# Feature and output rows written pair by pair from ScalarE's queue, gate logits made by node, and the last groups' VectorE steps in another order

## Chip, core and metric

The kernel runs on one core of one Trainium2 chip. The metric is the device time of one execution in microseconds (us). The profile of the kernel before is one execution of 2493.28 us, whose recorded span is 2491.6 us; the 1.7 us between them lie around the span.

## The reference

Three layers work on 6250 nodes with 256 features each: a graph convolution over 200,000 edges, a linear-attention block, and a mixture of eight experts. Only the last matters for the change. In short:

```python
xn = layernorm(x)
x = x + relu(gcn(edges, xn, W, b)) + mix(xn)          # called x2 in the kernel
h = layernorm(x)
logits = h @ gate_w + gate_b                          # 8 numbers per node
probs = softmax(logits); idx = argmax(probs)          # the expert of every node
pos = running count of the nodes of the same expert   # its place in the expert's list
kept = pos < 977                                      # 1.25 * 6250 / 8
y = relu(h @ w1[idx] + b1[idx]) @ w2[idx] + b2[idx]
out = x + y * probs[idx] * kept
```

## The kernel before

Nodes lie in 49 blocks of 128 (one node on each partition); the last block is partly padding. `acc` and `res` hold a block each in `[:, b, :]`.

**Edge stage.** 1563 chunks of 128 edges are processed in units of four. GpSimd gathers the source rows of a chunk with one indirect DMA (`ring<-node_rows,src_chunk`, L1026), SyncE counts a unit as ready when its rows have landed, TensorE multiplies it with a selection matrix (an item, L1087, two parts with other work between them), and VectorE adds the product to its block (`add`, L1662). An item is a unit and a block; there are 439. The last 49 items, numbered j = 0 to 48, each complete one block.

**Routing, inside those last 49 items.** As block b is complete, VectorE makes x2 (`x2`, L1809) and its statistics. For each pair t of blocks TensorE transposes x2 (`turn(t)`, L1204), ScalarE copies the result to `xT` (`copy`, L1458), and TensorE makes the gate logits. Before, these came out by expert (8 partitions by 256 nodes, `logits`, L1214), ScalarE copied them (`logits_out`, L1464), and TensorE transposed them to nodes (`logits_by_node`, L1224). ScalarE also scales x2 by dinv into `res` (`scale`, L1491); `res` then holds acc times dinv, 256 numbers, and three columns more of every node (`C:ROW`): minus mean over deviation, the inverse deviation, and the expert's probability.

Blocks are in groups, `RB = [0, 14, 28, 42, 49]`, group 0 to 3. For each group VectorE takes six `normal` steps (ending in two of the columns), eight `choose` steps (the expert), two `counted`, two `probability` steps (they need ScalarE's `exponent`, L1485, and end in the third column) and six `assign` steps: `cur`, `place`, `slot`, high and low part, `one_hi`, `one_lo`, `node_of`. `assign` needs the counts from TensorE (`places`, L1237 to L1245), and is followed there by `owners` (L1257), which puts node numbers into lists by expert. The steps of group g are taken at fixed gaps between the adds of group g+1; the table `STEPS` has the gap of each (28 gaps with 14 blocks, 14 gaps with the last 7). Gap 2u stands ahead of the add of block u of the group, 2u+1 behind its x2. After the last add, group 3's own steps follow, with `assign` of group 2 between its `normal` steps. VectorE then turns the lists into row numbers (`slots_ok`, L2094 to L2101).

**Writes.** Rows of 259 numbers go to `node_features` (`rows_out`, group 0 and 1 from ScalarE's queue at L1564, group 2 and 3 from SyncE's at L993); x2 rows go to the output (`x2_out`, groups 0 to 2 from ScalarE's queue at L1570, group 3 from SyncE's, L999, after the first four gathers of expert 0). `dma_out` and `dma_x2` count them.

**Expert stage.** GpSimd waits for `slots_ok` and for all of `dma_out`, and gathers expert 0's rows in eight DMAs (`load_rows(0)`, L1034). Then it waits for all of `dma_x2`, sets paddings to zero (L1043 to L1046, counted by `pads`), since two of these tiles lie where `acc` and `res` were, and gathers expert 1's rows. TensorE transposes rows 0 to 3 (`transposes`, L1284), makes the first two blocks of products of expert 0 (L1302) from the first half of its rows with the transposes of rows 4 to 7 between, and waits for `pads` ahead of the third block. From there to the end the eight experts run in one chain of TensorE, ScalarE and VectorE.

## Time and profile before

| | before |
|---|---|
| three runs, median (lowest to highest) | 2497.04 us (2495.24 to 2499.4) |
| profiled execution, its own time | 2493.28 us |
| its span | 2491.6 us |
| TensorE / TensorE weight loads busy | 1891.6 us (76%) / 1490.8 us (60%) |
| GpSimd busy | 1689.7 us (68%) |
| VectorE busy | 1210.4 us (49%) |
| ScalarE busy | 826.8 us (33%) |

Busy times are sums over the whole span and overlap each other. The edge stage takes the time to about 2058 us; the expert stage starts with GpSimd's first row gather at 2090.52 us and goes on to the end. The change works between these two points and around them.

### The profile page before, as it was taken

What the parts mean: (1) busy time and instruction counts of PE and PEld (TensorE: products, weight loads), DVE (VectorE), ACT (ScalarE), POOL (GpSimd) and SP (SyncE); (2) the same over time, 40 slices, a digit from 0 to 9 for tenths busy, and PEclk for the clock granted to TensorE, in tenths of its full rate; (3) what the DMA queues carried; (4) which work ended last, traced back from release to release, by engine and by line L of the source; (5) the groups of instructions that cost most, each with busy time, mean ns of one, the idle gap of its engine ahead of it and who ended that gap; (6) DMA issues with size and microseconds to landing.
All of it is one profiled execution on the core that took longest, in us unless ns stands there. A gap on an engine that the chain in (4) does not pass through costs nothing. (4 is left out here: it accounts for less than half of the span.)

```text
span 2491.6 us, 33433 instructions
## 1 busy us (share of the span) xinstructions
PE 1891.6 (76%) x8818; PEld 1490.8 (60%) x8818; DVE 1210.4 (49%) x3211; ACT 826.8 (33%) x1649; POOL 1689.7 (68%) x1780
## 2 busy tenths in 40 slices
PE   8588888677676776676777777777767775999997
PEld 7355555556555555555565555555544443998997
DVE  6333322344444444444444444444334554887886
ACT  5322222133333333233333333233201224565653
POOL 6577777777777777777777777777777772333432
PEclk9798999888988988889888888888879887999999
DMA  7433333333333333333333333333334446222320
GB/s 236 149 105 106 104 106 106 106 105 105 106 106 105 105 106 106 106 106 105 105 106 106 105 106 106 106 105 106 106 106 134 127 154 185 78 66 87 91 76 9
DMA packets 128044, 270.94 MB, mean 109 GB/s; under 512 B 33576, under 2 KB 71428, under 8 KB 127738
## 3 DMA queue, kind: packets, MB, share of 16 engines
q0 software_dynamic: 82992, 221.52, 31.0%
q1 hardware_dynamic: 35834, 38.11, 4.9%
q10 hardware_dynamic: 9040, 9.22, 1.2%
q8 instruction: 78, 1.28, 0.2%
q14 instruction: 100, 0.82, 0.1%
HBM read 244.15 MB, written 27.35 MB: 109 GB/s over the span
## 5 line engine op out<-in xcount | busy, mean ns | idle before, releaser
L1026 POOL DMA_INDIRECT ring<-node_rows,src_chunk x1563 | 1485.4, 950 | 491.7 <-issue 475.8
L1087 PE MATMUL p_item<-ring,sel 128*128 x3512 | 1010.4, 428 | 537.9 <-SPq L973 487.9
L1087 PEld LDWEIGHTS p_item<-ring,sel 128*128 128x128 f32 x3512 | 691.3, 210 | 767.9 <-issue 686.7
L1662 DVE TENSOR_TENSOR acc<-acc,p_item 128x256 f32 (+1 forms) x439 | 183.5, 418 | 620.0 <-PE p_item L1087 616.1
L1644 DVE SCALAR_TENSOR_TENSOR sel<-dst_chunk,nbase,p_col 128x512 f32<-128x512 f32 x439 | 326.5, 744 | 54.9 <-issue 36.9
L1052 POOL DMA_INDIRECT out_dram<-oo,slot_node x64 | 75.1, 1173 | 225.5 <-DVE oo L2006 222.6
L1391 ACT ACTIVATE x1T<-p_t,col_ln1b,col_ln1g 128x128 f32<-128x128 f32 x98 | 39.5, 453 | 333.7 <-PE p_item L1087 333.7
L1398 ACT ACTIVATE gT<-p_t,col_b 128x128 f32<-128x128 f32 x98 | 30.6, 363 | 315.0 <-PE p_item L1087 315.0
L1742 DVE SCALAR_TENSOR_TENSOR kf<-p_q,ke 128x256 f32<-128x256 f32 x49 | 20.8, 424 | 222.6 <-ACT ke L1373 222.6
L1034 POOL DMA_INDIRECT rows<-node_features,slot_row x64 | 73.0, 1141 | 54.7 <-DMA node_features<-res 35.7
L1150 PE MATMUL p_q<-wq_sb,xnT_m 128*128 128x512 f32 x196 | 108.6, 682 | 0.3
L1366 ACT ACTIVATE yn<-p_q 128x256 f32<-128x256 f32 x49 | 18.8, 383 | 228.2 <-PE p_item L1087 228.2
L1124 PEld LDWEIGHTS p_t<-x1T,w1t_sb 128*128 128x128 f32 x392 | 74.4, 266 | 5.4
L1302 PE MATMUL p_item<-bTh,w1h 128*128 128x490 f32 (+1 forms) x192 | 74.6, 389 | 4.0 <-DVE bTl L1953 2.1
L1423 ACT COPY xnT_m<-p_t 128x256 f32<-128x256 f32 x49 | 18.2, 372 | 176.2 <-PE p_item L1087 176.2
L2014 DVE TENSOR_TENSOR hTl<-hbuf,hTh 128x978 fp32r<-128x978 f32 x64 | 75.4, 1178 | 2.2
L1316 PE MATMUL p_col<-w2h,hTh 128*128 128x256 f32 x256 | 75.6, 295 | 0.8 <-DVE hTl L2014 0.7
L1316 PE MATMUL p_y<-w2h,hTh 128*128 128x256 f32 x256 | 74.7, 292 | 0.0
L1302 PE MATMUL p_item<-bTh,w1l 128*128 128x490 f32 (+1 forms) x192 | 74.3, 387 | 0.0
L1302 PE MATMUL p_item<-bTl,w1h 128*128 128x490 f32 (+1 forms) x192 | 73.8, 385 | 0.0
L1124 PE MATMUL p_t<-x1T,w1t_sb 128*128 128x128 f32 x392 | 73.5, 350 | 0.0
L1316 PE MATMUL p_y<-w2h,hTl 128*128 128x256 f32 x256 | 72.5, 283 | 0.0
(276 smaller groups left out, 3239.1 us busy)
## 6 DMA issues: line engine op xcount, KB each, us to landing
ring<-node_rows,src_chunk POOLq DMA_INDIRECT x1563, 2.8
w1raw<-in_w SPq DMA_DIRECT2D x8, 1024.0 KB, 5.4
w2raw<-in_w SPq DMA_DIRECT2D x8, 1024.0 KB, 6.7
res<-in_x SPq DMA_DIRECT2D x7, 896.0 KB, 9.7
out_dram<-res ACTq DMA_DIRECT2D x3, 1792.0 KB, 11.1
node_rows<-acc SPq DMA_DIRECT2D x4, 1024.0 KB, 4.9
node_features<-res ACTq DMA_DIRECT2D x2, 1813.0 KB, 9.7
node_features<-res SPq DMA_DIRECT2D x1, 1813.0 KB, 10.4
```

What stands on the lines that cost most here:

```text
L1026: nc.gpsimd.indirect_dma_start(ring[:, c % RING // U, c % U, :], None, table, bass.IndirectOffsetOnAxis(src_chunk[:, c:c + 1], 0)).then_in ...
L1034: nc.gpsimd.indirect_dma_start(rows[0:r, e % 2, t, :], None, feats, bass.IndirectOffsetOnAxis(slot_row[0:r, k:k + 1], 0)).then_inc((gather ...
L1052: nc.gpsimd.indirect_dma_start(out, bass.IndirectOffsetOnAxis(slot_node[0:r, k:k + 1], 0), oo[0:r, t % 2, :], None, bounds_check=N - 1, oo ...
L1087: mm = pe.matmul(p_item[bank(i)][:, 0:C], sel[:, i % SELR, u, :], rows[:, u, :], start=(u == 0), stop=(u == U - 1), skip_group_check=True)
L1124: pe.matmul(p_t[:, m, :], w1t_sb[:, a, m * P:(m + 1) * P], x1T[:, a, :], start=(a == 0), stop=(a == CH - 1))
L1150: pe.matmul(p_kv, xnT[:, a, :], wq_sb[:, a, C:3 * C], start=(a == 0), stop=(a == CH - 1))
L1302: mm = pe.matmul(e_f[c % 4][:, 0:NH[h]], w[:, a, j * P:(j + 1) * P], b[:, a, h * NH[0]:h * NH[0] + NH[h]], start=(q == 0), stop=(q == len( ...
L1316: mm = pe.matmul(e_y[t % 2][:, 0:C], h[:, j, t * P:(t + 1) * P], w[:, j, :], start=(q == 0), stop=(q == len(parts) - 1))
L1391: nc.scalar.activation(x1T[:, a, :], p_t[:, a, :], ACT.Identity, scale=g["cols"]["ln1g"][:, a:a + 1], bias=g["cols"]["ln1b"][:, a:a + 1]). ...
L1644: nc.vector.scalar_tensor_tensor(sel[:, i % SELR, :, :], dst.rearrange("p (u e) -> p u e", e=1).broadcast_to([P, U, P]), nbase[:, bass.ds( ...
L1662: nc.vector.tensor_tensor(a, a, p_item[bank(j)][:, 0:C], ALU.add).then_inc(added, 1)
L2014: V.tensor_tensor(hTl[:, j, 0:CAPE], hbuf[:, j % NBUF, :], hTh[:, j, 0:CAPE].bitcast(F32), ALU.subtract).then_inc(lo_ok, 1)
```

## The change

1. **Writes.** The 256 scaled numbers of a row and its three columns are written apart. Pairs 0 to 19 (blocks 0 to 39) go from ScalarE's queue, right behind their `scale`, each as two DMAs of 256 rows of 1024 bytes: to `node_features` and to the output. Blocks 40 to 43 and 44 to 48 go to `node_features` from SyncE's queue. The three columns go in one DMA for each group (12 bytes a node), group 0 and 1 from ScalarE's queue, 2 and 3 from SyncE's. The output rows of blocks 40 to 48 (before: 42 to 48) go from SyncE after all eight gathers of expert 0 (before: four).
2. **Logits.** Each block's transposed x2 is the stationary side of the matmul, with the gate weights (8 columns) moving, so that logits come out by node; the copy and the second transpose go.
3. **Order.** `STEPS` changes, `places(2)` moves ahead of TensorE's last item, and `assign` of group 2 moves ahead of VectorE's last add. `places` stands ahead of an item, not inside it. ScalarE takes `root` ahead of `scale`, group 2's `exponent` two pairs sooner, and `node_low(2)` ahead of the last scales.
4. **Waits.** ScalarE's wait for `dma_out` and `dma_x2` moves from the start of expert 0 to its first copy of w2; VectorE gets the same wait ahead of expert 0.

```diff
-    PLACES_AT = [RB[gi + 1] + 9 for gi in range(NG - 2)]
+    LATE_PAIR = 20
+    NFEAT, NX2 = LATE_PAIR + NG + 2, LATE_PAIR + 1
+    PLACES_AT = [min(RB[gi + 1] + 9, NBLK - 1) for gi in range(NG - 1)]
-        14: ((0, 1, 2, 3, 4, 5), (7, 8, 8, 9, 9, 10, 10, 11), (12, 12), (13, 13), ()),
+        14: ((0, 3, 4, 4, 5, 6), (6, 6, 7, 7, 8, 8, 8, 9), (10, 10), (13, 13), (12, 12, 12, 12, 12, 12)),
...
             sp.wait_ge(multiplied, NITEM)
-            rows_out(NG - 2)
+            rows_out(2 * LATE_PAIR, NBLK - 5)
             load_w2(sp, 0)
...
-            rows_out(NG - 1)
-            for t in range(RT // 2):
+            columns_out(NG - 2)
+            rows_out(NBLK - 5, NBLK)
+            columns_out(NG - 1)
+            for t in range(RT):
                 sp.wait_ge(gathered[t], rows_gathered(t) + 16)
-            x2_out(NG - 1)
+            sp.dma_start(out[2 * LATE_PAIR * P:NBLK * P, :].rearrange("(b p) c -> p b c", p=P),
+                         res[:, 2 * LATE_PAIR:NBLK, 0:C]).then_inc(dma_x2, 16)
...
             pool.wait_ge(slots_ok, 2)
-            pool.wait_ge(dma_out, 16 * NOUT)
+            pool.wait_ge(dma_out, 16 * NFEAT)
             load_rows(0)
-            pool.wait_ge(dma_x2, 16 * NOUT)
+            pool.wait_ge(dma_x2, 16 * NX2)
...
                 for i, b in enumerate(blocks_of(t)):
                     u = b - RB[gi]
-                    pe.transpose(p_l[:, u * EXP:(u + 1) * EXP], lgT[:, t % 2, i * P:(i + 1) * P],
-                                 ident[0:EXP, 0:EXP]).then_inc(l_ps, 1)
+                    for a in range(CH):
+                        mm = pe.matmul(p_l[:, u * EXP:(u + 1) * EXP], xT[:, t % XT, i * CH + a, :], gate_sb[:, a, :],
+                                       start=(a == 0), stop=(a == CH - 1))
+                    mm.then_inc(l_ps, 1)
...
+            def x2_out(t):
+
+                lo, hi = blocks_of(t)[0], blocks_of(t)[-1] + 1
+                s.wait_ge(scaled, hi)
+                s.dma_start(feats[lo * P:hi * P, 0:C].rearrange("(b p) c -> p b c", p=P), res[:, lo:hi, 0:C]
+                            ).then_inc(dma_out, 16)
+                s.dma_start(out[lo * P:hi * P, :].rearrange("(b p) c -> p b c", p=P), res[:, lo:hi, 0:C]
+                            ).then_inc(dma_x2, 16)
+
+            def columns_out(gi):
 
                 s.wait_ge(cols_ok, 3 * gi + 3)
-                s.wait_ge(scaled, RB[gi + 1])
-                s.dma_start(feats[RB[gi] * P:RB[gi + 1] * P, :].rearrange("(b p) c -> p b c", p=P),
-                            res[:, blocks(gi), :]).then_inc(dma_out, 16)
+                with nc.allow_non_contiguous_dma("three numbers of every node"):
+                    s.dma_start(feats[RB[gi] * P:RB[gi + 1] * P, C:ROW].rearrange("(b p) c -> p b c", p=P),
+                                res[:, blocks(gi), C:ROW]).then_inc(dma_out, 16)
...
+            node_low(NG - 2)
             scale(NPAIR - 2)
             scale(NPAIR - 1)
-            node_low(NG - 2)
...
                 normal(NG - 1, i)
-                assign(NG - 2, i)
...
+            v.wait_ge(dma_out, 16 * NFEAT)
+            v.wait_ge(dma_x2, 16 * NX2)
             all_experts(v, expert)
```

VectorE, from its last add (L1662) on, in the kernel before. `psum_e` is the first `probability` step of group 2, `veps` the first `normal` step of group 3, `cur` and `place_r` are the first `assign` steps of group 2, `inv` is group 3's.

```order
L1662 TENSOR_TENSOR acc<-acc,p_item 128x256 [waits added,multiplied]
L1814 BN_STATS stt<-acc 128x6 [waits r_x2]
L1818 BN_AGGR mvg<-stt 128x2 [waits r_bn]
L1809 SCALAR_TENSOR_TENSOR acc<-acc,res 128x256 [waits added]
L1895 TENSOR_REDUCE psum_e<-ex 128x14 [waits r_eact]
L1898 RECIPROCAL res<-psum_e 128x14 [waits r_dv]
L1814 BN_STATS stt<-acc 128x6 [waits r_x2]
L1818 BN_AGGR mvg<-stt 128x2 [waits r_bn] x2
L1826 SCALAR_TENSOR_TENSOR veps<-deg_1199,mvg 128x7 [waits r_dv]
L1906 TENSOR_TENSOR cur<-oh,p_nd 128x112 [waits r_oh,r_cum]
L1829 RECIPROCAL inv<-sdg 128x7 [waits r_std]
L1910 TENSOR_REDUCE place_r<-cur 128x14 [waits r_dv]
```

VectorE in the changed kernel, from the x2 of block 47 on. The add is the same one, now at L1650.

```order
L1894 TENSOR_TENSOR cur<-oh,p_nd 128x112 [waits r_oh,r_cum]
L1898 TENSOR_REDUCE place_r<-cur 128x14 [waits r_dv]
L1901 SCALAR_TENSOR_TENSOR slot_r<-place_r,m_1208 128x14 [waits r_dv]
L1905 TENSOR_SCALAR slot_hi<-slot_r 128x14 [waits r_dv]
L1906 TENSOR_SCALAR slot_lo<-slot_r 128x14
L1910 TENSOR_TENSOR one_hi_r<-col,slot_hi 128x896 [waits r_mapped,r_dv]
L1913 TENSOR_TENSOR one_lo_r<-col,slot_lo 128x1792
L1916 TENSOR_TENSOR node_of<-one_hi_r,node_hi 128x14x64 [waits r_onehi]
L1650 TENSOR_TENSOR acc<-acc,p_item 128x256 [waits added,multiplied]
L1802 BN_STATS stt<-acc 128x6 [waits r_x2]
L1806 BN_AGGR mvg<-stt 128x2 [waits r_bn]
L1797 SCALAR_TENSOR_TENSOR acc<-acc,res 128x256 [waits added]
```

All of group 2's `assign` steps now stand ahead of the last add; before, the first came after it, and behind `veps` of group 3.

ScalarE, from the copy of the last transposes on, in the kernel before. `sdg` is `root(3)`, `node_of` is `node_low(2)`, `ex` is `exponent(3)`, and an ACT_TABLE_LOAD changes the function table.

```order
L1458 COPY xT_r<-p_t 128x256 [waits r_lt,r_turned]
L1464 COPY lgT<-p_item 8x256 [waits r_lps,r_lt]
L1480 ACT_TABLE_LOAD
L1480 ACTIVATE sdg<-veps 128x7 [waits r_var]
L1464 COPY lgT<-p_item 8x128 [waits r_lps,r_lt]
L1491 ACTIVATE res<-acc,dinv 128x256 [waits r_x2] x3
L1471 ACTIVATE node_of<-one_hi_r,node_lo 128x14x64 [waits r_mapped,r_onehi]
L1511 CAST w1h<-w1raw 128x512 [waits d_w1,multiplied]
L1485 ACT_TABLE_LOAD
L1485 ACTIVATE ex<-ex 128x56 [waits r_e]
```

ScalarE in the changed kernel, at the same place.

```order
L1452 COPY xT_r<-p_t 128x256 [waits r_lps,r_turned]
L1468 ACT_TABLE_LOAD
L1468 ACTIVATE sdg<-veps 128x7 [waits r_var]
L1459 ACTIVATE node_of<-one_hi_r,node_lo 128x14x64 [waits r_mapped,r_onehi]
L1479 ACTIVATE res<-acc,dinv 128x256 [waits r_x2] x3
L1499 CAST w1h<-w1raw 128x512 [waits d_w1,multiplied]
L1473 ACT_TABLE_LOAD
L1473 ACTIVATE ex<-ex 128x56 [waits r_e]
```

Two copies of logits are gone; `node_low(2)` stands ahead of the three scales.

SyncE after the last unit, in the kernel before (`w1raw` there is expert 1's).

```order
L993 DMA node_features<-res 128x14x259 [waits multiplied,r_scaled,r_cols]
L960 DMA w2raw<-in_w 128x8x256
L1005 DMA fb_b<-in_fb 128x2048
L993 DMA node_features<-res 128x7x259 [waits r_scaled,r_cols]
L999 DMA out_dram<-res 128x7x256 [waits gathered3,gathered2,r_scaled,gathered1,gathered0]
L957 DMA w1raw<-in_w 128x2x1024 [waits e_w1l]
```

SyncE in the changed kernel, at the same place.

```order
L994 DMA node_features<-res 128x4x256 [waits multiplied,r_scaled]
L962 DMA w2raw<-in_w 128x8x256
L1007 DMA fb_b<-in_fb 128x2048
L1001 DMA node_features<-res 128x14x3 [waits r_cols]
L994 DMA node_features<-res 128x5x256 [waits r_scaled]
L1001 DMA node_features<-res 128x7x3 [waits r_cols]
L1014 DMA out_dram<-res 128x9x256 [waits gathered4,gathered5,gathered3,gathered6,gathered2,gathered7,gathered1,gathered0]
L959 DMA w1raw<-in_w 128x2x1024 [waits e_w1l]
```

The last feature write of 7 whole rows is now 5 rows and 7 times three numbers, and the output write waits for four more gathers.

## Rows read from the trace of the kernel before

**Rows 1.** The page's costliest groups: the gathers of the edge stage (columns in the page's order)

```profile
L1026 POOL DMA_INDIRECT ring<-node_rows,src_chunk x1563 | 1485.4, 950 | 491.7 <-issue 475.8
```

**Rows 2.** Timeline: two gathers and TensorE's item behind each, an output write (start, us)

```profile
1855.20 0.95 POOL L1026 DMA_INDIRECT ring<-node_rows,src_chunk  x1 [0.30 <-issue]
...
1858.16 2.07 PE L1087 MATMUL p_item<-ring,sel 128*128 x4 [1.97 <-SPq L973]
...
2052.74 0.38 ACTq L1570 DMA_DIRECT2D out_dram<-res  x1
...
2053.90 0.95 POOL L1026 DMA_INDIRECT ring<-node_rows,src_chunk  x1 [0.30 <-issue]
...
2058.50 2.07 PE L1087 MATMUL p_item<-ring,sel 128*128 x4 [5.94 <-SPq L973]
```

**Rows 3.** Stretches: busy time of each engine, granted TensorE clock, DMA share, GB/s

```profile
2054.00:2058.00 4.00, 0.00 (x0) 0.00 (x0) 0.94 (x5) 0.00 (x0) 0.85 (x1) 0.67 1.05 275
2058.00:2062.00 4.00, 3.50 (x8) 1.55 (x8) 0.00 (x0) 0.00 (x0) 0.00 (x0) 0.50 1.08 391
```

**Rows 4.** Timeline from the x2 of block 47 to the first row gather

```profile
2065.05 0.40 DVE L1809 SCALAR_TENSOR_TENSOR acc<-acc,res 128x256 f32<-128x256 f32 x1
...
2066.76 0.42 DVE L1662 TENSOR_TENSOR acc<-acc,p_item 128x256 f32<-128x256 f32 x1 [0.54 <-PE p_item L1087]
...
2067.52 0.39 DVE L1809 SCALAR_TENSOR_TENSOR acc<-acc,res 128x256 f32<-128x256 f32 x1
...
2068.48 0.55 PE L1241 MATMUL p_nd<-oh,ones 128*128 128x104 bf16 x13
...
2070.35 0.38 SPq L993 DMA_DIRECT2D node_features<-res  x1
...
2072.09 1.28 ACT L1480 ACT_TABLE_LOAD   x1
...
2073.62 0.20 DVE L1829 RECIPROCAL inv<-sdg 128x7 f32<-128x7 f32 x1 [2.47 <-ACT sdg L1480]
...
2075.33 1.09 DVE L1922 TENSOR_TENSOR one_hi_r<-col,slot_hi 128x896 bf16<-128x896 f32 x1
...
2078.43 1.09 DVE L1928 TENSOR_TENSOR node_of<-one_hi_r,node_hi 128x896 bf16<-128x896 bf16 x1
2079.43 0.21 DVE L1853 TENSOR_TENSOR lg<-p_q,inv 128x56 f32<-128x56 f32 x1
...
2081.25 0.20 DVE L1895 TENSOR_REDUCE psum_e<-ex 128x7 f32<-128x56 f32 x1
...
2081.72 0.37 SPq L993 DMA_DIRECT2D node_features<-res  x1
...
2086.97 0.23 DVE L2101 SCALAR_TENSOR_TENSOR slot_node<-node_f,gone 128x64 int32<-128x64 f32 x1
...
2090.52 0.94 POOL L1034 DMA_INDIRECT rows<-node_features,slot_row  x1 [35.67 <-DMA node_features<-res]
```

**Rows 5.** DMA issues: count, KB each, median us from issue to landing

```profile
node_features<-res SPq DMA_DIRECT2D x1, 1813.0 KB, 10.4
...
node_features<-res SPq DMA_DIRECT2D x1, 906.5 KB, 8.1
out_dram<-res SPq DMA_DIRECT2D x1, 896.0 KB, 5.3
...
first<-in_dstF SPq DMA_DIRECT2D x1, 6.5 KB, 2.9
```

**Rows 6.** Timeline: last gather of expert 0, first and last padding, third block of products

```profile
2099.27 0.99 POOL L1034 DMA_INDIRECT rows<-node_features,slot_row  x1 [0.31 <-issue]
...
2102.64 0.10 POOL L1043 MEMSET bTh<- 128x2 f32 x1 [2.37 <-DMA out_dram<-res]
...
2103.05 0.41 POOL L1046 MEMSET hTl<- 128x368 f32 x1
...
2108.31 0.46 PE L1302 MATMUL p_item<-bTh,w1h 128*128 128x488 f32 x1 [0.84 <-DVE bTl L1953]
```

More of the change, by code:

```diff
@@ L1207, in logits @@
             def logits(t):
-                k = len(blocks_of(t))
+                gi = next(i for i in range(NG) if 2 * t < RB[i + 1])
                 t_.wait_ge(xT_ok, t + 1)
@@ L1211, in logits @@
                     t_.wait_ge(centred, CH)
-                wait(t_, lt_sb, t)
-                for a in range(CH):
-                    mm = pe.matmul(p_lt[0:EXP, 0:k * P], gate_sb[:, a, :], xT[:, t % XT, a:k * CH:CH, :],
-                                   start=(a == 0), stop=(a == CH - 1))
-                mm.then_inc(lt_ps, 1)
-            def logits_by_node(t):
-                gi = next(i for i in range(NG) if 2 * t < RB[i + 1])
-                t_.wait_ge(lt_sb, t + 1)
                 wait(t_, lg_ok, gi)
@@ L1270, in route @@
                         means()
-                if not odd and 1 <= t <= NPAIR:
-                    logits_by_node(t - 1)
                 for gi in range(NG - 2):
-                    if j == PLACES_AT[gi]:
-                        places(gi)
                     if j == OWNERS_AT[gi]:
@@ L1325, in _ @@
             for j in range(NBLK):
+                for gi in range(NG - 1):
+                    if j == PLACES_AT[gi]:
+                        places(gi)
                 item(0, 2 * (ROUTE0 + j))
@@ L1328, in _ @@
                 item(0, 2 * (ROUTE0 + j) + 1)
-            route(NBLK)
             turn(NPAIR - 2)
-            logits_by_node(NPAIR - 3)
-            places(NG - 2)
+            logits(NPAIR - 3)
             turn(NPAIR - 1)
             logits(NPAIR - 2)
-            logits_by_node(NPAIR - 2)
             logits(NPAIR - 1)
-            logits_by_node(NPAIR - 1)
             owners(NG - 2)
@@ L1515, in high_w2 @@
                     s.wait_ge(d_w2, e * 16 + 16)
+                    if isinstance(e, int) and e == 0:
+                        s.wait_ge(dma_out, 16 * NFEAT)
+                        s.wait_ge(dma_x2, 16 * NX2)
                     wait(s, f2_ps, e * RT)
@@ L1558, in expert, with columns_out @@
                 keep_sign(e, RT - 2)
-            def rows_out(gi):
-                s.wait_ge(cols_ok, 3 * gi + 3)
-                s.wait_ge(scaled, RB[gi + 1])
-                s.dma_start(feats[RB[gi] * P:RB[gi + 1] * P, :].rearrange("(b p) c -> p b c", p=P),
-                            res[:, blocks(gi), :]).then_inc(dma_out, 16)
-            def x2_out(gi):
-                s.wait_ge(scaled, RB[gi + 1])
-                s.dma_start(out[RB[gi] * P:RB[gi + 1] * P, :].rearrange("(b p) c -> p b c", p=P),
-                            res[:, blocks(gi), 0:C]).then_inc(dma_x2, 16)
+            def x2_out(t):
+                lo, hi = blocks_of(t)[0], blocks_of(t)[-1] + 1
+                s.wait_ge(scaled, hi)
+                s.dma_start(feats[lo * P:hi * P, 0:C].rearrange("(b p) c -> p b c", p=P), res[:, lo:hi, 0:C]
+                            ).then_inc(dma_out, 16)
+                s.dma_start(out[lo * P:hi * P, :].rearrange("(b p) c -> p b c", p=P), res[:, lo:hi, 0:C]
+                            ).then_inc(dma_x2, 16)
+            def columns_out(gi):
+                s.wait_ge(cols_ok, 3 * gi + 3)
+                with nc.allow_non_contiguous_dma("three numbers of every node"):
+                    s.dma_start(feats[RB[gi] * P:RB[gi + 1] * P, C:ROW].rearrange("(b p) c -> p b c", p=P),
+                                res[:, blocks(gi), C:ROW]).then_inc(dma_out, 16)
             key_rows(0)
```

46 lines of the change are left out of this document (16 added, 30 removed).

## The prediction

> **What bounds the kernel now.** First the page's groups: GpSimd's gathers take 1485.4 us of 1563 issues, and of the 491.7 us it stood idle ahead of them 475.8 are its own issue gap [rows 1]. For most of the 2491 us one thing thus sets the pace, a gather every 1.25 us. The change adds nothing to GpSimd's queue there, and hardly any idle time is left that another engine's wait could explain. So the copies, matmuls and VectorE steps that go or move inside the edge stage are worth nothing: work waits for rows there, as the last item waited 5.94 us for SyncE's ready count [rows 2].
>
> Second, the timeline at the seam of the stages, read backwards from GpSimd's first row gather at 2090.52. Its idle time of 35.67 us ended with the write of the last features [rows 4], issued at 2081.72 and landed 8.1 us later, at 2089.8 [rows 4, 5]: 0.7 us from landing to start. The lists it also needs were complete at 2087.20 [rows 4]. So two chains end there, the write and 2.6 us ahead of it the lists, and both go back to the last unit of edges.
>
> Third, the stage behind. TensorE's third block of products starts at 2108.31, 17.8 us after the first row gather, when the last rows are in [rows 4, 6]. From there all experts hang in one chain. The change is worth the shift of 2090.52 plus that of these 17.8 us.
>
> **The last unit.** The last item started 4.6 us after the issue of the last gather (2053.90 to 2058.50), an undisturbed one 2.96 us (1855.20 to 1858.16) [rows 2]. Between them lies bulk: a group of output rows issued at 2052.74 [rows 2], and a DMA share of 1.05 and 1.08 in those stretches [rows 3]. With pairs written as they come, ScalarE's last pair is pair 19, several items sooner, and only gathers are left. Gain 4.6 less 2.96, 1.6 us; bounds 0 and 1.6, I take 1.6. The Trainium skill (DMA: Bandwidth & Descriptors, the table of rules at its end) says that spreading DMAs over SP, ACT and GpSimd gives no bandwidth, since all run on the same 16 engines and interleave. By that the other queue alone would give nothing and only the earlier time counts; the share of 1.05 agrees.
>
> **The lists.** Every time 1.6 earlier, in the order of the changed program:
> - x2 of block 47 ended at 2065.45 [rows 4], now 2063.85. All of group 2's `assign` follows. Its three large steps took from 2075.33 to 2079.52, 4.2 us; four small ones ahead, twice as wide as `lg` with its 0.21, about 0.9 [rows 4]. So 5.1 us, to 2069.0. `places(2)` (0.55 and a first and last matmul, some 0.7 [rows 4]) moves ahead of the last item and puts it back by as much; the add doesn't feel it, since it now waits for VectorE.
> - The last add is thus at 2069.0, not 2066.76: 2.2 later. This is the price of the order. Queued behind it are the last x2, the transposes of the last block, ScalarE's copy, its table load and `root(3)`. x2 is 0.76 behind the add and takes 0.4 [rows 4], to 2070.1; transposes and copy 0.9: table load at 2071.0. It was at 2072.09, since copies of logits stood ahead of it in ScalarE's queue. From load to `inv` it took 1.53 (2072.09 to 2073.62 [rows 4]): now 2072.5, 1.1 sooner.
> - From `inv` to `lg` it was 5.8 us (2073.62 to 2079.43 [rows 4]), with the large `assign` steps between. Without them it is some five small steps, 1.1 us: `lg` at 2073.6, 5.8 sooner. Not all of it arrives, as ScalarE is late next: behind the root stand `node_low(2)`, three scales, a piece of w1, the table load of 1.28 and the exponent, some 4.4 us in all, to 2076.9. `psum_e` waits for that: 2076.9 for 2081.25.
> - From there to the end of `slot_node` it was 5.95 us (2081.25 to 2087.20 [rows 4]), unchanged: lists at 2082.8, GpSimd 0.7 later at 2083.5. Against 2090.52 that is 7.0 us; without the gain at the last unit 5.4.
>
> **The writes.** Before, SyncE's queue moved 1.86, 1.05, 1.05 and 0.93 MB (group 2's rows, w2, the experts' last bias, group 3's rows) from 2070.35 to 2089.8 [rows 4, 5]: 4.9 MB, 250 GB/s with all starts and landings. Now it has 0.52, 1.05, 1.05 and 0.66 MB from the last item on, about 2066.4: 3.28 MB, at the same rate to 2079.5. The columns come on top, 1792 and 896 runs of 12 bytes. No store this small is in the trace. From below: the load `first`, 1664 single numbers, landed 2.9 us after its issue [rows 5], so at most 1.7 ns each and 4.7 us for 2688; part of the 2.9 is fixed. From above: 1792 whole rows landed in 10.4 us [rows 5], 5.8 ns each, so 15.6 us. The writes then end by 2084.2, or at 2095.1, and GpSimd starts at 2083.5 (the lists) to 2084.9, or at 2095.8. Twelve bytes are far nearer to four than to 1036: I take 3.8 us and 2084.0. Gain 6.5.
>
> **Behind the first row gather.** The output write of the last blocks now waits for eight gathers, not four. The last is issued 8.75 us after the first [rows 4, 6]; with 2.96 to land it is there at +11.7. The write took 5.3 us for 896 KB [rows 5]; for 1152 KB it lands at +17.0 (same time) to +18.5 (in proportion). Queued behind GpSimd's wait for it are the paddings, 0.8 us (2102.64 to 2103.46 [rows 6]), and for these TensorE's third block waits: +17.9 to +19.4, where it was +17.8 and waited for rows that had met this same write. Cost 0.1 to 1.6 us, I take 0.8. TensorE also stands idle some 3.5 us ahead of the block. After its idle 5.94 us at the last unit the granted clock was 0.50, the lower of its two levels (1.2 GHz), through all of 2058 to 2062 [rows 2, 3]; four us at half speed cost 2. Bounds 0 and 2, I take 1.4, the idle time being shorter. GpSimd's gathers for expert 1 start 5 us later and are needed far behind: nothing. The moved waits of ScalarE and VectorE end when the write has landed, ahead of their work: nothing.
>
> **Sum.** 6.5 less 0.8 less 1.4 is 4.3 us less: the profiled execution of 2493.28 (span 2491.6 and 1.7 around it) would be 2489.0. It is 3.8 below the median of the runs shown, so from 2497.04 the forecast is **2492.7 us**. A measurement of this kernel tells about 0.2%, 5.0 us, from no change; the sum lies just within.
>
> **The rivals.**
> - *Small writes are dear*, ending on the other side. The whole gain is eaten when the columns take 8.1 us, 3.0 ns a run (GpSimd at 2088.3, with 2.2 behind it). At the row's 5.8 ns GpSimd starts 5.3 late, and the time is 7.5 more, 2504.5; more than 5.0 is lost from 4.9 ns on. For it: they are stores to DRAM, and the queue that ends last carries them. Against: 1664 loads cost 2.9 us. It would also come about if each number travelled by itself, 8064 at up to 1.7 ns, 13.7 us, GpSimd at 2093.9 and the time 2502.6. The Trainium skill (DMA: Bandwidth & Descriptors, the table of rules) says that a strided last dimension becomes one descriptor per element; here three neighbours lie in it, and no row tells which it is. Time 2495 to 2505, chance 0.24, of it 0.11 beyond 5.0.
> - *The padding wait costs nothing*: the write lands after 5.3 again, the clock stays up or VectorE sets expert 0's pace anyway. 6.5 to 7.3 less, 2490. For it: the write no longer shares with gathers. Chance 0.22.
> - *The forecast*, 2490.5 to 2495: 0.46.
> - *The order frees less*: TensorE, idle ahead of the last block's transposes and logits, runs them slowly, or the last item stays at 2058.5. The lists gain 3 less, 1.3 less in all, 2495.7. Chance 0.08.
>
> **How the numbers follow.** Faster by over 5.0: the second rival and 0.2 of the forecast's share, 0.42. Slower by over 5.0: 0.11 and a rest, 0.12. Within: 0.46. The range goes from 2487.5 (7.3 less and 2 of scatter) to 2500.5, into the dear case, and leaves 2 in 10 out. The likeliest case alone has 2490.5 to 2495.
>
> **What would show it.** The last item's start at 2056.9; the last add behind `node_of` of group 2, near 2069; `psum_e` held by ScalarE to about 2077; lists at 2082.8. GpSimd's first row gather at 2083.5 to 2085, released by `slot_node` or the column write; past 2088 small writes are dear. Expert 0's rows landing evenly, paddings ending at +18 to +19.5, the third block right behind them at a clock of 0.5. The forecast is wrong if the columns take over 8 us, if the last item stays at 2058.5, or if the block is held past +20.

## The result, and the profile after

| | before | after |
|---|---|---|
| seven runs each, median (lowest to highest) | 2497.4 us (2495.24 to 2501.8) | 2487.87 us (2486.76 to 2492.0) |
| profiled execution, its own time | 2493.28 us | 2492.0 us |
| its span | 2491.6 us | 2490.3 us |

The ratio is 0.9963, with a 95% interval of 0.9954 to 0.9973: 9.2 us less (6.7 to 11.5). The forecast was 4.3 less. The two profiled executions differ by only 1.3 us. The one of before is below all seven of its timed runs, and the one of after is the highest of its seven; in it, the first gather of the edge stage came 2.3 us later (95.87 against 93.61). So times below are counted from a near event, not from the start of the span.

The timeline of the changed kernel at the last units (start, us):

```profile
2052.24 0.95 POOL L1031 DMA_INDIRECT ring<-node_rows,src_chunk  x1 [0.30 <-issue]
...
2056.00 0.99 POOL L1031 DMA_INDIRECT ring<-node_rows,src_chunk  x1 [0.30 <-issue]
...
2056.84 2.07 PE L1092 MATMUL p_item<-ring,sel 128*128 x4 [2.77 <-SPq L975]
...
2063.62 0.83 PE L1240 MATMUL p_nd<-oh,ones 128*128 128x104 bf16 x13
...
2066.24 1.03 PE L1092 MATMUL p_item<-ring,sel 128*128 x4
```

The item that waited for rows starts 0.84 us after the last gather's issue, where it was 4.60 [rows 2]. The last item's second half, at 2066.24, is 10.24 behind that issue, where it was 11.69 (2065.59 less 2053.90). Between the first and the last gather of the edge stage nothing changed: 1960.1 us (95.87 to 2056.00), where it was 1960.3.

The same timeline to the first row gather:

```profile
2068.99 1.09 DVE L1916 TENSOR_TENSOR node_of<-one_hi_r,node_hi 128x896 bf16<-128x896 bf16 x1
2069.99 0.41 DVE L1650 TENSOR_TENSOR acc<-acc,p_item 128x256 f32<-128x256 f32 x1
...
2072.05 1.28 ACT L1468 ACT_TABLE_LOAD   x1
2073.58 0.20 DVE L1817 RECIPROCAL inv<-sdg 128x7 f32<-128x7 f32 x1 [1.30 <-ACT sdg L1468]
2074.65 0.21 DVE L1841 TENSOR_TENSOR lg<-p_q,inv 128x56 f32<-128x56 f32 x1
...
2077.78 0.21 DVE L1883 TENSOR_REDUCE psum_e<-ex 128x7 f32<-128x56 f32 x1 [1.24 <-ACT ex L1473]
...
2078.26 0.39 SPq L1001 DMA_DIRECT2D node_features<-res  x1
...
2083.17 0.22 DVE L2088 SCALAR_TENSOR_TENSOR slot_node<-node_f,gone 128x64 int32<-128x64 f32 x1
2085.43 1.20 POOL L1039 DMA_INDIRECT rows<-node_features,slot_row  x1 [28.44 <-DMA node_features<-res]
```

The last add stands behind `node_of`, `psum_e` waits for ScalarE's `ex`, the lists end at 2083.39, and the column write still ends the wait. From the last gather's issue to the first row gather: 29.43 us, where it was 36.62 [rows 2, 4]. That is 7.2 sooner. The last column write is issued 22.3 us behind the last gather, as soon as its columns are there (before: 27.8), and takes 6.4 us to land (before: 8.1 [rows 5]).

Behind it:

```profile
2098.09 0.38 SPq L1014 DMA_DIRECT2D out_dram<-res  x1
...
2101.39 0.32 DVE L1941 TENSOR_TENSOR bTl<-p_q,bTh 128x162 fp32r<-128x162 f32 x1
2103.69 0.10 POOL L1048 MEMSET bTh<- 128x2 f32 x1 [8.25 <-DMA out_dram<-res]
...
2104.09 0.40 POOL L1051 MEMSET hTl<- 128x368 f32 x1
2104.55 0.78 PE L1297 MATMUL p_item<-bTh,w1h 128*128 128x488 f32 x1 [3.80 <-POOL hTl L1051]
```

And by stretches (busy time of PE, PEld, DVE, ACT, POOL, then granted clock, DMA share, GB/s):

```profile
2104.00:2108.00 4.00, 3.45 (x9) 2.87 (x10) 0.00 (x0) 0.60 (x1) 3.23 (x5) 0.50 0.69 247
2108.00:2112.00 4.00, 4.00 (x16) 3.35 (x15) 3.27 (x4) 1.92 (x4) 3.08 (x4) 0.78 0.30 88
```

The last of `bTl`, all that the third block needs besides paddings, is ready at 2101.71, +16.3 from the first row gather. The block starts at +19.1, released by a padding, after 3.8 us of idle TensorE, and runs at 0.50 (1.2 GHz). From the first row gather to the end of the span it is 404.9 us, where it was 401.1: 3.8 given back. In these two executions the change thus brings 7.2 less 3.8, or 3.4, behind the last gather, and most of the measured 9.2 is not in them.

### The profile page after: what moved, and what is told of

Same layout as the page of the kernel before. It is cut to its first block, busy times and chain, and to the rows that moved or that the text cites. A ratio compares the mean times of both kernels' runs of the same rounds, so it can differ in the third digit from the quotient of the medians.

```text
span 2490.3 us, 33494 instructions
## 1 busy us (share of the span) xinstructions
PE 1896.4 (76%) x8865; PEld 1521.0 (61%) x8865; DVE 1210.3 (49%) x3211; ACT 818.6 (33%) x1624; POOL 1691.8 (68%) x1780
## 4 chain that ended last, share of the span: by engine, by line
POOL 60%; issue 20%; PE 14%; DMA 1%; DVE 1%; ACT 0%; DVEq 0%; ACTq 0%; POOLq 0%; SPq 0%
POOL ring L1031 59%; PE p_item L1297 4%; PE p_y L1311 4%; PE p_col L1311 3%; PE p_nd L1297 2%; DVE hTh L2000 0%; POOL rows L1039 0%; DMA node_features<-res 0%; DMA out_dram<-oo,slot_node 0%; DMA out_dram<-res 0%; PE p_t L1279 0%; PE p_q L1279 0%; DMA ring<-node_rows,src_chunk 0%; DVE hTl L2002 0%; PE p_item L1092 0%
## 5 line engine op out<-in xcount | busy, mean ns | idle before, releaser
L1092 PE MATMUL p_item<-ring,sel 128*128 x3512 | 1029.7, 434 | 533.0 <-SPq L975 490.8
L1092 PEld LDWEIGHTS p_item<-ring,sel 128*128 128x128 f32 x3512 | 704.3, 215 | 760.1 <-issue 675.8
L1650 DVE TENSOR_TENSOR acc<-acc,p_item 128x256 f32 (+1 forms) x439 | 183.3, 418 | 618.4 <-PE p_item L1092 614.5
L1360 ACT ACTIVATE yn<-p_q 128x256 f32<-128x256 f32 x49 | 18.8, 384 | 227.9 <-PE p_item L1092 227.9
L1452 ACT COPY xT_r<-p_t 128x512 f32<-128x512 f32 (+1 forms) x25 | 14.4, 578 | 206.4 <-PE p_t L1209 206.4
L1417 ACT COPY xnT_m<-p_t 128x256 f32<-128x256 f32 x49 | 18.2, 372 | 191.3 <-PE p_item L1092 191.3
L1528 ACT ACTIVATE hbuf<-p_item,fb_sb 128x490 f32<-128x490 f32 (+1 forms) x96 | 62.9, 671 | 31.2 <-PE p_item L1297 21.7
```

Source lines behind the costliest of these rows:

```text
L1092: mm = pe.matmul(p_item[bank(i)][:, 0:C], sel[:, i % SELR, u, :], rows[:, u, :], start=(u == 0), stop=(u == U - 1), skip_group_check=True)
L1528: nc.scalar.activation(hbuf[:, j % NBUF, h * NH[0]:h * NH[0] + NH[h]], e_f[c % 4][:, 0:NH[h]], ACT.Relu, bias=fb1_sb[:, bass.ds(e, 1), j]) ...
L1650: nc.vector.tensor_tensor(a, a, p_item[bank(j)][:, 0:C], ALU.add).then_inc(added, 1)
```

## The experiments

Twelve kernels, four on each of three other chips (A, B, C). There both kernels take some 2880 to 2920 us: the first gather of the edge stage comes about 50 us later, and from the first to the last it takes 328 to 353 us longer (last part of this document). So ratios to the kernel before on the same chip are compared, and stretches behind the last item. Only chip B has the changed kernel beside its variants; between chips, ratios are compared only roughly. "Less" and "more" in us are the ratio and its 95% interval times the median of before on that chip.

| kernel | chip | ratio (95%) | us against before |
|---|---|---|---|
| pads_split | A | 0.9953 (0.9939 to 0.9966) | 13.6 less (9.8 to 17.7) |
| out_after_4 | A | 0.9952 (0.9939 to 0.9965) | 13.9 less (10.1 to 17.7) |
| old_order | A | 0.9991 (0.9977 to 1.0004) | 2.6 less (6.7 less to 1.2 more) |
| whole_rows | A | 1.0 (0.9986 to 1.0014) | 0 (4 less to 4 more) |
| after_again | B | 0.9969 (0.9954 to 0.9984) | 9.0 less (4.7 to 13.4) |
| pads_split_b | B | 0.995 (0.9935 to 0.9964) | 14.5 less (10.5 to 18.9) |
| columns_twice | B | 0.9968 (0.9956 to 0.9981) | 9.3 less (5.5 to 12.8) |
| logits_only | B | 1.0015 (0.9998 to 1.0033) | 4.4 more (0.6 less to 9.6 more) |
| before_again | C | 0.9995 (0.9983 to 1.0007) | 1.5 less (5.0 less to 2.0 more) |
| out_after_4_b | C | 0.9959 (0.9945 to 0.9973) | 12.0 less (7.9 to 16.0) |
| split_and_4 | C | 0.9959 (0.9944 to 0.9973) | 12.0 less (7.9 to 16.3) |
| before_split_8 | C | 0.9987 (0.9973 to 1.0001) | 3.8 less (7.9 less to 0.3 more) |

From each one's profile, in us: from the start of the last item's second half to the start of `slot_node` (the end of the lists) and to the first row gather, with what released it; from there to the third block of products and to the end of the span. (In before, that second half starts at 2065.59.)

| kernel | lists | first row gather | third block | to the end |
|---|---|---|---|---|
| before | 21.4 | 24.9, write | 17.8 | 401.1 |
| before_again | 21.4 | 24.9, write | 18.3 | 403.1 |
| logits_only | 19.6 | 23.9, write | 19.9 | 406.0 |
| whole_rows | 18.0 | 25.7, write | 19.8 | 406.4 |
| before_split_8 | 21.4 | 24.5, write | 16.8 | 400.2 |
| old_order | 19.6 | 20.1, lists | 19.4 | 404.3 |
| after | 16.9 | 19.2, write | 19.1 | 404.9 |
| after_again | 18.0 | 18.5, lists | 19.3 | 404.1 |
| columns_twice | 17.9 | 20.9, write | 18.8 | 404.7 |
| pads_split, pads_split_b | 17.9, 18.2 | 19.8 write, 18.7 lists | 16.3, 15.9 | 399.4, 399.1 |
| out_after_4, out_after_4_b | 18.2, 17.9 | 19.3, 19.0, write | 19.8, 19.8 | 403.4, 403.1 |
| split_and_4 | 18.2 | 19.5, write | 20.1 | 403.2 |

### What lies ahead of the last item on chips A, B and C

after_again was expected to take 0.37% less than before, with the first row gather at 19.2 us, the third block at +19.1 and 386 us behind it. It took 0.31% less, with 18.5, +19.3 and 384.8. But the same total is made up in another way. On the first chip the last item's second half starts 11.7 us (before) and 10.2 (after) behind the last gather's issue. On these chips it is 17.7 to 32.6: the gathers are done, and TensorE works off items that wait for VectorE. A wait for the add among the last items, in before_again and then in after_again:

```profile
2471.03 2.07 PE L1087 MATMUL p_item<-ring,sel 128*128 x4 [3.47 <-DVE acc L1662]
```

```profile
2462.05 2.07 PE L1092 MATMUL p_item<-ring,sel 128*128 x4 [1.66 <-DVE acc L1650]
```

So here the new order of the steps can bring time ahead of the last item, and it seems to. From the x2 of block 0 to the last item's second half, the four profiles with the old order take 248.2 to 253.9 us, mean 251.6, and the eight with the new one 238.9 to 249.5, mean 244.4. (On the first chip it is 223.4 before and 221.7 after.) The timed runs agree. The profiles give what each kernel gains behind the start of that second half, against 427.0 us, the mean of before and before_again there. What the timed gain has beyond this is 4.6 to 9.6 us in all eight kernels with the new order, and between 1.5 less and 2.5 more in the four with the old one. No run isolates it, and single profiles scatter. But it says that times on these chips hold some 5 to 10 us that come with the new order ahead of the last item, where the first chip shows only 1.5. The readings below therefore go by the stretches, not by the times alone.

### pads_split and pads_split_b: paddings apart

```diff
             load_rows(0)
-            pool.wait_ge(dma_x2, 16 * NX2)
             if CAPE > CAP:
                 nc.gpsimd.memset(bTh[...], 0.0).then_inc(pads, 1)
                 nc.gpsimd.memset(bTl[...], 0.0).then_inc(pads, 1)
+            pool.wait_ge(dma_x2, 16 * NX2)
...
-                    if first and c == 2:
-                        t_.wait_ge(pads, 4 if CAPE > CAP else 2)
+                    if first and c == 2 and CAPE > CAP:
+                        t_.wait_ge(pads, 2)
...
+                    if first and t == 0:
+                        t_.wait_ge(pads, 4 if CAPE > CAP else 2)
```

> The changed kernel with only the two small paddings (bTh, bTl) ahead of GpSimd's wait for the output write, and TensorE's third block of products waiting for these two alone; the paddings of hTh and hTl stay behind the write and are waited for ahead of the second products. Theory A, the padding wait costs: in the changed kernel the third block started 19.1 us after the first row gather, while the last bTl was ready at +16.3 (2101.71 against 2085.43); TensorE stood idle 3.8 us and then ran 5 us at 0.50. Without that wait the block starts at about +16.5 and the clock stays up: 3 to 5 us less than the changed kernel, about 2484. Rival B, expert 0 is paced by VectorE and ScalarE anyway (the wait costs nothing): within 1 us of the changed kernel, about 2487.5.

> The kernel with the two small paddings ahead of the wait once more, beside the unaltered changed kernel. Theory A (the padding wait and the clock behind it cost 4 to 5.5 us): 4 to 5.5 us less than the changed kernel on this chip, third block at +16.3. Rival B: part of it is given back in the eight experts, and no more than 2 us are left.

The timeline of pads_split_b, with its first row gather at 2497.59:

```profile
2507.61 0.12 POOL L1048 MEMSET bTl<- 128x2 f32 x1
...
2510.52 0.38 SPq L1014 DMA_DIRECT2D out_dram<-res  x1
...
2513.00 0.32 DVE L1943 TENSOR_TENSOR bTl<-p_q,bTh 128x162 fp32r<-128x162 f32 x1
2513.46 0.46 PE L1297 MATMUL p_item<-bTh,w1h 128*128 128x488 f32 x1 [1.10 <-DVE bTl L1943]
```

The third block is released by `bTl`, at +15.9, and a matmul of 488 columns takes 0.46 us, not 0.78. From the first row gather to the end, its two profiles have 399.4 and 399.1 us; the four kernels whose block waits for the write of nine blocks have 404.9, 404.1, 404.7 and 404.3, mean 404.5. Theory A holds in the profiles: the wait and the clock behind it cost about 5 us, 3.1 of them (19.2 less 16.1, means) the wait. The times say the same, less firmly: on the chip of both, the changed kernel is 9.0 less than before and this one 14.5, with intervals that overlap. Against the kernel before it is clearly faster on both chips.

### out_after_4, out_after_4_b and split_and_4: the output write sooner

```diff
-            for t in range(RT):
+            for t in range(RT // 2):
                 sp.wait_ge(gathered[t], rows_gathered(t) + 16)
```

split_and_4 has this and the edit above.

> The changed kernel with the output write of nine blocks behind the first four gathers of expert 0, as in the kernel before, not behind all eight. Theory A: the write is issued 4 to 5 us sooner and lands at about +14, but it shares the DMA engines with the last gathers, so that the third block starts at about +17.8 as before, waiting for rows: 1 to 2.5 us less than the changed kernel, about 2486. Rival B (the padding wait costs nothing): no difference, within 1 us. Rival C: the gathers are held so long by 1.15 MB that the block starts later than +19: 1 us more.

> The changed kernel with the output write behind four gathers once more, for a firm size. Theory A (the paddings come sooner, the rows later, the block no sooner; only the clock gains): 1 to 2 us less than the changed kernel, 3 to 4 more than the one with the paddings split; 403 us from the first row gather to the end. Rival B: 4 us less than the changed kernel, as the ratio to the kernel before on the other chip had it.

> The changed kernel with both: the two small paddings ahead of the wait and the output write behind four gathers. Theory A (with the paddings split, nothing waits for the output write any more, while its bytes hold up the last four row gathers): the third block comes at +19.8 for lack of rows, 403 to 404 us from the first row gather to the end, 3 to 4 us more than with the paddings split alone. Rival B, the write hides in either place: 399 to 400 us.

The timeline of out_after_4_b, with its first row gather at 2500.51; `xe` is ScalarE's first reading of a block of gathered rows, here the sixth:

```profile
2507.35 0.38 SPq L1014 DMA_DIRECT2D out_dram<-res  x1
2507.77 0.74 SPq L959 DMA_DIRECT2D w1raw<-in_w  x1
...
2514.87 0.60 ACT L1486 ACTIVATE xe<-rows 128x256 f32<-128x256 f32 x1 [5.37 <-DMA rows<-node_features,slot_row]
2515.09 0.10 POOL L1048 MEMSET bTh<- 128x2 f32 x1 [4.56 <-DMA out_dram<-res]
```

The paddings now come at +14.6, but ScalarE stands 5.37 us before rows that travel beside this write and the load of expert 1's w1 (1024 KB) that SyncE issues 0.4 us behind it; no run parts the two. The block comes at +19.8, not at the +17.8 that theory A of out_after_4 had: that is rival C's late block, without the microsecond of loss it named. TensorE is at full clock there (383.3 us from the block to the end, as with the paddings apart). In the profiles that leaves 1.3 us of gain, theory A's size. The ratios of 0.9952 and 0.9959, beside 0.9969 on another chip, say 3 to 5 us less than the changed kernel, with intervals of 4 to either side, so rival B of out_after_4_b isn't excluded by time. The clearest reading is split_and_4: 403.2 us, just as with the write alone moved, and 4 more than with the paddings alone. Once no padding waits for the write, it and the load behind it do harm beside the gathers. Theory A holds there, by the profiles; the ratios of 0.9959 and 0.995 overlap.

### old_order and whole_rows: one chain shortened at a time

old_order is the changed kernel with the old `STEPS`, `places(2)` behind the last item, and the old orders of VectorE and ScalarE:

```diff
-        14: ((0, 3, 4, 4, 5, 6), (6, 6, 7, 7, 8, 8, 8, 9), (10, 10), (13, 13), (12, 12, 12, 12, 12, 12)),
+        14: ((0, 1, 2, 3, 4, 5), (7, 8, 8, 9, 9, 10, 10, 11), (12, 12), (13, 13), ()),
...
                 normal(NG - 1, i)
+                assign(NG - 2, i)
```

whole_rows is the changed kernel with the writes of before:

```diff
-            rows_out(2 * LATE_PAIR, NBLK - 5)
+            rows_out(NG - 2)
             load_w2(sp, 0)
...
-            columns_out(NG - 2)
-            rows_out(NBLK - 5, NBLK)
-            columns_out(NG - 1)
-            for t in range(RT):
+            rows_out(NG - 1)
+            for t in range(RT // 2):
```

> The changed kernel with the old table of steps, places(2) behind the last item, assign of group 2 behind the last add, and ScalarE's old order; the new writes and logits stay. Theory A, the order frees what the prediction said: the lists are complete about 4.4 us later against the last item, and they end last, so that GpSimd's first row gather comes 3 to 4.5 us later than in the changed kernel (there 29.4 us after the last gather's issue; here 32.5 to 34): about 2491. Rival B, the column write ends the wait whatever the order, since its bytes set the time: within 1 us of the changed kernel, 2488.

> The changed kernel with the writes of the kernel before (whole rows of 259 numbers by group, output by group, the last output write after four gathers); the new order and the new logits stay. Theory A, the writes are the bound: 4.9 MB still follow the last item in SyncE's queue at about 250 GB/s, so the last one lands hardly sooner than before, and GpSimd's first row gather stands 35.5 to 36.6 us after the last gather's issue: 2494.5 to 2497.5. Rival B, the last write only waits for its columns: these are ready 4.4 us sooner, the write lands as much sooner, first row gather at 32 us: about 2492.5.

The timeline of whole_rows, whose last item's second half starts at 2459.74:

```profile
2472.81 0.37 SPq L994 DMA_DIRECT2D node_features<-res  x1
2477.73 0.23 DVE L2081 SCALAR_TENSOR_TENSOR slot_node<-node_f,gone 128x64 int32<-128x64 f32 x1
2485.39 0.95 POOL L1035 DMA_INDIRECT rows<-node_features,slot_row  x1 [49.57 <-DMA node_features<-res]
```

Its last write is issued 13.1 us behind the last item (16.1 in before) and still lands no sooner: GpSimd starts at 25.7, and 7.4 us after the lists. So the bytes ahead of this write set its end, not the three columns it waits for; rival B falls and theory A holds. The time is that of the kernel before; but behind the last item it is 5 us more (432.1 from the second half's start to the end, against 427.0), and the order made up for that ahead of it.

In old_order the lists end the wait, at 19.6, 0.5 us ahead of the gather, as theory A had it. Its size was not: the lists are 1.4 to 1.7 us later than in the eight kernels of these chips with the new order (17.9 to 18.2), not 4.4, and the gather, at 20.1, is 0.3 to 1.6 later than in those of them that have the new writes without a second column write (18.5 to 19.8), not 3 to 4.5. The 1.8 us from 21.4 to 19.6 come with the logits by node, as logits_only shows.

At this wait the two parts are thus worth: the order without the writes nothing (25.7 against 24.9), the writes without the order 4.8 us (20.1, with the new logits), both together 5.1 to 6.4. The order counts there only once the write is out of the way. In time, whole_rows and old_order are 0 and 2.6 us less (6.7 less to 1.2 more) than before and after_again 9.0, but these hold what lies ahead of the last item too, and the intervals of 0 and 2.6 overlap.

### columns_twice: the price of small stores

```diff
             rows_out(NBLK - 5, NBLK)
+            sp.dma_start(spare[RB[NG - 2] * P:RB[NG - 1] * P, C:ROW].rearrange("(b p) c -> p b c", p=P),
+                         res[:, blocks(NG - 2), C:ROW]).then_inc(dma_out, 16)
             columns_out(NG - 1)
```

> The changed kernel, and SyncE writes group 2's three columns a second time, to another tensor, ahead of group 3's columns; GpSimd waits for that as well. It measures the disputed price of the small stores: 1792 more runs of 12 bytes in the queue that ends last. Theory A (a run costs 1.4 ns, as the prediction took it): first row gather 2.5 us later than in the changed kernel. Rival B (a run costs what a whole row cost, 5.8 ns): 10.4 us later. Rival C (the queue is not what ends it, a DMA has a fixed time to land): less than 1 us.

The page's queues of this kernel, SyncE's (packets, MB, share), and then those of after_again:

```profile
q1 hardware_dynamic: 39082, 36.82, 4.2%
```

```profile
q1 hardware_dynamic: 37274, 36.79, 4.1%
```

The 1792 runs of 12 bytes are 1808 packets more: one for a run, with 16 to spare, and not one for a number. The Trainium skill (DMA: Bandwidth & Descriptors, Why a DMA increments its semaphore by 16 and not by 1) says that a descriptor moves one contiguous run of the last dimension; this agrees, and the table of rules on the same page, by which a strided last dimension becomes one per element, is no rule for this store, whose last dimension is three neighbours and strided only from row to row. The first row gather is 1.1 to 1.9 us later than in the four kernels of these chips with the new writes and order whose wait the write ended (19.0 to 19.8), 0.6 to 1.0 ns a run; in two more the lists ended the wait (18.5 and 18.7), which tells only that the write was there by then. The time is that of after_again, within some 4 us. Theory A had 2.5 us, rival C less than 1: it lies between them. Rival B, 10.4 us, is out; so is the prediction's rival of dear small writes.

### logits_only and before_again

logits_only is the kernel before with the logits by node and the moved waits of ScalarE and VectorE. before_again is the kernel before, unaltered.

> The kernel before with only the logits made by node and the moved waits of ScalarE and VectorE; order and writes as before. Theory A (copies, transposes and waits inside the edge stage are worth nothing): the time of the kernel before within 0.1%, first row gather 24 to 25.5 us after the last item's second half. Rival B: two copies less in ScalarE's queue ahead of the last root bring 1 us or more.

> The kernel before once more, unaltered, for a second profile of it. Theory A, the profiled execution on which the forecast rested was an unusually good one (2493.28 us, below each of its seven timed runs): there TensorE's clock came up at +12.5 and 401.1 us passed from the first row gather to the end. Two later kernels with the same writes and the same expert stage took 406.4 and 406.0, with the third block at +19.8 and a clock of 0.50 into it. The second profile shows 405 to 407 us and a third block at +19 to +20. Rival B, the 401 us are the rule and the moved waits of ScalarE and VectorE made the other two slow: 401 to 402 us again.

logits_only has its lists 1.8 us sooner behind the last item and its row gathers 1.0 sooner, at 23.9, just past theory A's 24 to 25.5 and at the 1 us of rival B. In time nothing of it is seen (0.6 us less to 9.6 more). before_again showed 403.1 us behind the first row gather, not 401.1, and not the 405 to 407 that theory A named either. Its stretch at the third block, which starts at 2527.72:

```profile
2527.00:2531.00 4.00, 3.28 (x9) 2.73 (x10) 0.48 (x2) 1.93 (x4) 2.96 (x4) 0.61 0.39 88
```

The clock is 0.61 there, mostly the lower level, where the execution behind [rows 6] ran the block's matmuls at full speed from 2108.31. So the unaltered kernel has 401.1 and 403.1 us in this stage, mean 402.1. logits_only and whole_rows have 406.0 and 406.4. Is that the same scatter? ScalarE's wait for the sixth block of rows speaks against it, here in before_again:

```profile
2520.64 0.60 ACT L1498 ACTIVATE xe<-rows 128x256 f32<-128x256 f32 x1 [2.58 <-DMA rows<-node_features,slot_row]
```

It is 2.16 us in before and 2.58 in before_again; in the five other kernels with the output write behind four gathers (logits_only, whole_rows, out_after_4, out_after_4_b, split_and_4) it is 5.23 to 5.56. In all seven the write goes out at +6.6 to +6.8 and the load of w1 0.4 us later. And where one code has two profiles, the stage differs by 0.3 (pads_split), 0.3 (out_after_4), 0.8 (after) and 2.0 us (before). So the late rows go with the code. The five share the logits by node and the moved waits of ScalarE and VectorE; rival B of before_again, that the moved waits made the two slow, is not ruled out. In the program these waits stand behind the reading of expert 0's rows, and how they could hold the rows up is not shown. No run has the one without the other and the write behind four gathers.

### before_split_8: the stage behind the seam alone

```diff
             load_rows(0)
-            pool.wait_ge(dma_x2, 16 * NOUT)
...
+            pool.wait_ge(dma_x2, 16 * NOUT)
             nc.gpsimd.memset(hTh[...], 0.0).then_inc(pads, 1)
...
-            for t in range(RT // 2):
+            for t in range(RT):
                 sp.wait_ge(gathered[t], rows_gathered(t) + 16)
```

> The kernel before with nothing of the change but this: the output write behind all eight gathers, the two small paddings ahead of the wait for it, and the moved waits of ScalarE and VectorE that go with it. Theory A (in the kernel before the expert stage loses some 7 us to rows that are held up by this write, and to the clock behind them): 399 to 400 us from the first row gather to the end, 6 to 7 us less than the kernel before. Rival B: the stage behind the seam is paced by other work, 2 us or less.

(TensorE's two edits of pads_split and the moved waits of ScalarE and VectorE belong to it.) It has 400.2 us to the end, close to theory A's 399 to 400, with the block at +16.8. The time is 3.8 less (7.9 less to 0.3 more), not 6 to 7. That size had been reckoned from 406.0 and 406.4, which are not the kernel before's: against its own 401.1 and 403.1 the stage is 0.9 and 2.9 shorter. So with the moved waits in it and the write behind eight gathers the rows are not late (a wait of 1.37 us).

## Why the prediction was right and wrong

Its range held the time by 0.4 us (2487.87, with the lower end at 2487.5; its own terms, 2497.04 less 9.3, give 2487.7), and the sum in it was half of the measured gain. Step by step, in times from the last gather's issue (2053.90 before, 2056.00 after):

- **What bounds it.** Right: two chains end at the first row gather, the write and the lists. old_order and whole_rows showed each by itself. That work inside the edge stage is worth nothing is right on the first chip (1960.3 and 1960.1 us from the first gather to the last), but not a property of the kernel: on the other three its last items wait for VectorE.
- **The last unit.** The sum was nearly right, the reading wrong. The prediction counted 4.6 us from the last gather to the waiting item, and took this item for the last; it is the one of block 47, the last but one. In the changed kernel that item starts 0.84 us after the last gather, when the gather's rows can't be there (2.8 us is their median): it waits for the unit ahead, whose last gather was issued at 2052.24. So it stood 8.3 us behind its own rows' gather before (2050.16 to 2058.50), and 4.6 now. It is 3.8 sooner, not 1.6. TensorE gave 2.3 back, for it ran the logits, `owners` and items behind it slowly (the half item at 2061.72 took 2.02 us, the last one 1.03), and `places(2)` (1.0) now lies ahead of the last item; the last item's second half is 1.45 sooner.
- **The lists.** Forecast and measured, from the last gather's issue: last add 15.1 and 14.0, table load 17.1 and 16.05, `inv` 18.6 and 17.6, `lg` 19.7 and 18.65, `psum_e` 23.0 and 21.8 held by ScalarE, end 28.9 and 27.4. All in the order and by the releasers named, a steady 1.0 to 1.5 us sooner. Of the 4.5 us by which the lists end sooner behind the last item (21.4 to 16.9), 1.8 come with the logits by node, as logits_only showed.
- **The writes.** Forecast 30.1 to the first row gather, measured 29.4. The working let the columns follow the bytes of the queue; in the trace the last column write is issued only when its columns are ready, 22.3 us behind the last gather, and lands 6.4 later. The 3.8 us taken for the columns was not measured as such; 0.6 to 1.0 ns a run would be 1.6 to 2.8 us for 2688.
- **Behind the first gather.** The wait: the block was put at +17.9 to +19.4, and is there at +19.1 (18.8 to 19.4 in four kernels). The clock: from the block to the end it is 385.8 us, and 383.1 to 383.6 where the clock stays up, so about 2.5, and 1.3 to 2.8 over the four, where 1.4 was taken with bounds of 0 and 2. For these two executions the terms sum to 7.2 less 3.8, 3.4, and the forecast was 4.3.
- **The sum.** It held in the traces. The execution costed is the better of two of its kernel in this stage (401.1 and 403.1), and the changed kernel, with its like, has a mean of 404.5. From the means the stage gives back 2.4 us, where 0.8 and 1.4 were taken, and 7.2 less 2.4 is 4.8, beside the forecast of 4.3.
- **What the sum does not have.** The timed gain is 9.2 us, 6.7 at the least. The forecast carried its 4.3 over with "It is 3.8 below the median of the runs shown", as if the changed kernel's profile would stand as far below its own median. It stands 4.1 above it, and that of before 4.1 below its median of seven. 2.3 of these 8.2 us are the later first gather, ahead of everything that changed. What the 4.8 lack to 9.2, 4.4 us (1.9 to 6.7), stays open: the two profiles don't have it, and the other chips can't settle it, since 5 to 10 us of their gain lie ahead of the last item. That the range held the time is in this part luck: its lower end had 7.3 us less, the terms at their most favourable, and 2 us of scatter.
- **The rivals.** Dear small writes: out, by columns_twice. That the padding wait costs nothing came nearest in time (2490), by the wrong mechanism: the wait costs 3 us and the clock 2, as pads_split showed. That the order frees less: not on the first chip, where the lists end 1.5 us sooner than forecast. On the other chips the order moves them by 1.4 to 1.7 us, beside 1.8 for the logits.

## What to carry to other kernels

Where two chains end at one wait, an edit to the one that ends sooner measures as nothing there (25.7 against 24.9), so try it again with the other shortened before dropping it. Ask of a profiled execution where it stands among its timed runs, and take a second profile of the same code before carrying a difference of a few us over: here same-code pairs differed by 0.3 to 2.0 us in one stage, and the two profiles compared stood 4.1 us to either side of their medians. When a gain is measured on another chip, check that the same stage ends last there; an equal ratio (0.9963 and 0.9969) can have another make-up. A wait placed on one buffer for the sake of another (here two columns of padding behind a write of 1.15 MB) costs its length and the clock behind it: wait for each where it is used.

## What was not expected of the hardware

- The same programs took 2495 us on the first chip and 2880 to 2920 on three others. There the edge stage is not paced by GpSimd's issue alone: in pads_split GpSimd waited 377.2 us for SyncE's count of free units, which waits in turn for TensorE to have multiplied them. VectorE's 501.0 us are for releasers that the profile doesn't name; on the first chip it waits 614.5 us for TensorE ahead of the same add, so these need not be time lost in addition. Some waits of pads_split (us in total, times, longest):

```profile
DVE acc L1652 <- remote: 501.0, 71, 14.3
POOL ring L1031 <- issue: 433.6, 1405, 1.9
POOL ring L1031 <- SPq L983: 377.2, 157, 6.5
```

  No run here shows the cause. Behind the last item, before_again has the same 21.4 and 24.9 us as before; the lists of the new order end 1.0 to 1.3 us later there (17.9 to 18.2) than on the first chip (16.9). `cur` of group 2 starts 1.3 us ahead of the last item's second half on the first chip, 0.3 to 0.5 on the others; that is most of it.
- TensorE at the third block: after 3.80 us of idle time its matmul of 488 columns took 0.78 us and the granted clock of the next 4 us was 0.50 (after). After 4.42 us idle the first took only 0.49, yet the clock fell behind it, to 0.69 over 2508 to 2512 (after_again). After 1.10 us idle it kept 0.46 (pads_split_b). The idle time right ahead is not the whole of it: after 0.84 us it was 0.46 in before, 0.62 in before_again and 0.75 in whole_rows.
- A write of 896 or 1152 KB, and 1024 KB of w1 right behind it, beside the gathers of 128 rows: ScalarE waited for the sixth of these 5.23 us in whole_rows and 5.37 in out_after_4_b, but 2.16 and 2.58 in before and before_again, and 1.18 to 1.40 where both come behind all eight.
